# One-hot matrices stored by the attention stage and loaded by the geometric stage, with their scaling on ScalarE

## The chip, the cores and the metric

The kernel runs on one NeuronCore of a Trainium2 chip. The metric is the device time of one execution in microseconds (us), the median of three runs. TensorE (PE) multiplies matrices, VectorE (DVE) and ScalarE (ACT) work elementwise, GpSimd (POOL) issues the gathers, SyncE (SP) issues plain DMAs. Each engine works through its own instructions in order and meets the others at semaphores. PEld in the profile is the weight load of TensorE.

## The reference, cut to what matters

A graph of 3125 nodes and 50000 edges, sorted by destination, goes through two message-passing layers with a feed-forward layer behind each. Both layers sum messages over the edges of each destination node:

```
# layer 0: attention
w   = softmax of scores over the edges of one dst
agg = segment_sum(w * V[src], dst)
# layer 1: geometric
h0, h1 = tensor product of lin(x[src]) with the edge's unit vector
sc   = leaky_relu(h0) @ lsc / 8
act  = softmax(concat([sc, zeros(192)]))        # 64 real logits and 192 zeros
msgs = act * concat([o0, o1])                   # 256 columns for each edge
agg  = segment_sum(msgs, dst)
x    = x + agg
```

## The kernel before, in words

Sorted edges lie in tiles of EP = 128; the edges of one tile all go to one tile of P = 125 nodes. A step takes U = 4 edge tiles, and there are STEPS = 104 steps. A stage sums an edge tile into its node tile by one product on PE: the messages (128 edges x 256 columns) are multiplied by a one-hot matrix (128 edges x 125 nodes) that has a one where the edge's destination is that node. DVE then adds the product to `agg` in SBUF.

`build_attention` is the first of the two stages. Its DVE makes the one-hot matrices of a step with one instruction over 128 x 500 elements (`one_hot`, L1236) into one of two buffers. This happens LAG steps behind the step whose scores it computes. SP loads one 256 KB row block for each step, R = 3 blocks ahead, each after the DVE instruction that frees its buffer (`make`, L1209).

`build_geometric` is the second. For step s, in the order of each engine:

- POOL issues four indirect gathers, 256 KB each, into one of R = 4 buffers `g_rows` (L1418). Before the gathers of step s it waits for `s_xm` of step s - 4.
- DVE, step s: `largest` and `negate` (L1536, L1540) on the logits of s; `projected` for step s + 2 (L1525), which waits for the gathers of s + 2; an addition of step s - 1's product (L1546); `lead` for s + 2 (L1531); an addition; `vec` (L1571), which waits for ACT's exponentials; the sum `rz` (L1577); an addition; `vec` again (L1582); the reciprocal of `rz` (L1585); an addition; `t1` (L1588); the four one-hot matrices of s with the factor `rz` in them (L1593); `msg` columns 0 to 63 (L1596).
- ACT, step s: `turned` for s + 1 (L1429); `exps` for s (L1439, L1441, L1444); `relu` for s + 1 (L1433); `scaled` for s (L1453), which waits for `vec` and ends with `s_xm`.
- PE, iteration s: transposes for s + 1 (L1472); first half of the product of s - 1 (L1500), which waits for `s_msg` and `s_xm` of s - 1; `hidden` for s + 1 (L1477); second half (L1500); `out` for s + 1 (L1486, L1490), on which `largest` of s + 1 waits.

SP has nothing to do in the geometric stage before the change.

Of the kernel before, what the change touches and what calls it, by code (L numbers as in the profile page):

```python
# [25 lines left out]
P = 125  # L26
# [968 lines left out]
def build_attention(nc, m, room):  # L995
# [4 lines left out]
    with ExitStack() as ctx:  # L1000
# [6 lines left out]
        def part(n):  # L1007
# [44 lines left out]
        s_ch = sem("a_ch")  # L1052
        s_w = sem("a_w")
        s_fac = sem("a_fac")
        block = ctx.enter_context(nc.Block())
        LINKS, CHAIN = 5, 18
        (XS, FWD, BWD, ENDS, FIRST, REACH, BACK, LEFT, RIGHT, MINE, DROP, OVER, DIAG, CC, FWD_L, BWD_R, TOP, LESS
         ) = range(1, CHAIN + 1)

# [26 lines left out]

        @block.sync
        def _(sp):
            for s in range(STEPS):
                if s >= R:  # L1090
                    sp.wait_ge(s_ht, s - R + 1)
                sp.dma_start(rowb[s % R][:, :], m.rows_d[s:s + 1, :].to_broadcast([128, 2 * W])
                             ).then_inc(s_row[s % R], 16)

        @block.scalar
        def _(act):
# [107 lines left out]
        def _(dve):  # L1204
# [28 lines left out]
            def one_hot(s):  # L1233
                if s >= 2:
                    dve.wait_ge(s_mm, U * (s - 1))
                dve.tensor_tensor(hot[s % 2][:, :, :], m.iota[:, None, 0:P].to_broadcast([EP, U, P]),  # L1236
                                  m.rec[:, s * U:s * U + U, R_LO:R_LO + 1].to_broadcast([EP, U, P]), ALU.is_equal
                                  ).then_inc(s_hot, 1)
# [121 lines left out]
def build_geometric(nc, m):  # L1360

    MW = D
    R = 4
    AHEAD = 2
    with ExitStack() as ctx:  # L1365
        sem = Sems(nc, ctx)

# [8 lines left out]
        ex = [sb(f"g_ex{b}", [EP, U, 64]) for b in range(2)]  # L1376
        z = [sb(f"g_z{b}", [EP, U]) for b in range(2)]
        en = [sb(f"g_en{b}", [EP, U]) for b in range(2)]
        rz = sb("g_rz", [EP, U])
        t1 = sb("g_t1", [EP, U, 64])  # L1380
        vec = [sb(f"g_vec{b}", [EP, U, 192]) for b in range(2)]
        hot = [sb(f"g_hot{b}", [EP, U, P]) for b in range(2)]
        msg = [sb(f"g_msg{b}", [EP, U, MW]) for b in range(2)]
        xr = sb("g_xr", [EP, U, 64, 3])
        ps_t = ctx.enter_context(nc.psum_tensor("g_pst", [128, U, EP], F32))
# [2 lines left out]
        ps_a = [ctx.enter_context(nc.psum_tensor(f"g_psa{k}", [P, 2, MW], F32)) for k in range(2)]  # L1388
        s_x = [sem(f"g_x_{r}") for r in range(R)]
        s_go = sem("g_go")  # L1390
        s_xr = sem("g_xr")
        s_y = sem("g_y")
        s_tr = sem("g_tr")
# [18 lines left out]
        def _(pool):  # L1412
# [9 lines left out]
            for s in range(STEPS):  # L1422
                gather(s, s % R)

        @block.scalar
        def _(act):
            def turned(s, b):
                act.wait_ge(s_tr, s + 1)
                act.activation(ut[b][:, :, :], ps_t[:, :, :], ACT.Copy).then_inc(s_ut, 1)  # L1429

            def relu(s, b):
                act.wait_ge(s_h, s + 1)
                act.activation(lk[b][:, :, :], ps_h[:, :, :], ACT.Relu).then_inc(s_lk, 1)  # L1433

            def exps(s, b):
                act.wait_ge(s_nm, s + 1)
                if s >= 2:
                    act.wait_ge(s_msg, s - 1)
                act.activation(en[b][:, :], nm[b][:, :], ACT.Exp)  # L1439
                for u in range(U):  # L1440
                    act.activation(ex[b][:, u, :], ps_o[b][:, u, 128:192], ACT.Exp, bias=nm[b][:, u:u + 1],  # L1441
                                   accum_out=z[b][:, u:u + 1])
                for u in range(U):
                    last = act.activation(t1[:, u, :], rows[s % R][:, u, 512:576], ACT.Copy,  # L1444
                                          scale=m.unit2[:, s * U + u:s * U + u + 1])
                last.then_inc(s_ex, 1)

            def scaled(s, b):
                act.wait_ge(s_vec, s + 1)
                if s >= 2:  # L1450
                    act.wait_ge(s_prod, 2 * s - 2)
                for u in range(U):
                    last = act.activation(msg[b][:, u, 64:256], vec[b][:, u, :], ACT.Copy, scale=en[b][:, u:u + 1])  # L1453
                last.then_inc(s_xm, 1)

            turned(0, 0)
            relu(0, 0)
            for s in range(STEPS):
                b = s % 2
                if s + 1 < STEPS:  # L1460
                    turned(s + 1, 1 - b)
                exps(s, b)
                if s + 1 < STEPS:
                    relu(s + 1, 1 - b)
                scaled(s, b)

        @block.tensor
        def _(pe):
            def turn(s, r):
                pe.wait_ge(s_y, s + 1)  # L1470
                for u in range(U):
                    last = pe.transpose(ps_t[:, u, :], rows[r][:, u, 0:128], m.ident[:, :])  # L1472
                last.then_inc(s_tr, 1)

            def hidden(s, b):
                pe.wait_ge(s_ut, s + 1)
                pe.matmul(ps_h.rearrange("p u e -> p (u e)"), m.w_h[:, :],  # L1477
                          ut[b].rearrange("p u e -> p (u e)"), start=True, stop=True).then_inc(s_h, 1)

            def out(s, b):  # L1480
                pe.wait_ge(s_ut, s + 1)
                if s >= 2:
                    pe.wait_ge(s_t1, s - 1)
                    pe.wait_ge(s_ex, s - 1)
                for u in range(U):
                    pe.matmul(ps_o[b][:, u, 0:192], ut[b][:, u, :], m.w_o[:, :], start=u % 2 == 0, stop=False,  # L1486
                              skip_group_check=True)
                pe.wait_ge(s_lk, s + 1)
                for u in range(U):
                    last = pe.matmul(ps_o[b][:, u, 128:192], lk[b][:, u, :], m.w_s[:, :], start=False, stop=True,  # L1490
                                     skip_group_check=True)
                last.then_inc(s_out, 1)

            def aggregate(s, b, k):
                if k == 0:
                    pe.wait_ge(s_msg, s + 1)
                    pe.wait_ge(s_xm, s + 1)
                pe.wait_ge(s_sum, s * U + 2 * k + 2)
                for u in (2 * k, 2 * k + 1):
                    last = pe.matmul(ps_a[k][:, u % 2, :], hot[b][:, u, :], msg[b][:, u, :], start=True, stop=True)  # L1500
                last.then_inc(s_prod, 1)

            turn(0, 0)
            hidden(0, 0)
            out(0, 0)
            for s in range(STEPS + 1):
                b = s % 2
                if s + 1 < STEPS:
                    turn(s + 1, (s + 1) % R)
                if s:  # L1510
                    aggregate(s - 1, 1 - b, 0)
                if s + 1 < STEPS:
                    hidden(s + 1, 1 - b)
                if s:
                    aggregate(s - 1, 1 - b, 1)
                if s + 1 < STEPS:
                    out(s + 1, 1 - b)

        @block.vector
        def _(dve):  # L1520
# [28 lines left out]
            def step(s, r):  # L1549
# [17 lines left out]
                if not last:  # L1567
                    dve.wait_ge(s_ex, s + 1)
                    if s >= 2:
                        dve.wait_ge(s_xm, s - 1)  # L1570
                    dve.tensor_tensor(vec[b].rearrange("p u (c k) -> p u c k", k=3),  # L1571
                                      ps_o[b][:, :, 64:128, None].to_broadcast([EP, U, 64, 3]),
                                      m.unit[:, ds(s * U, U), None, :].to_broadcast([EP, U, 64, 3]), ALU.mult
                                      ).then_inc(s_o01, 1)
                    if s:
                        dve.wait_ge(s_msg, s)
                    dve.scalar_tensor_tensor(rz[:, :], en[b][:, :], 192.0, z[b][:, :], ALU.mult, ALU.add  # L1577
                                             ).then_inc(s_rz, 1)
                add(2)
                if not last:  # L1580
                    dve.wait_ge(s_o01, s + 1)
                    dve.tensor_tensor(vec[b][:, :, :], vec[b][:, :, :], rows[r][:, :, 320:512], ALU.add  # L1582
                                      ).then_inc(s_vec, 1)
                    dve.wait_ge(s_rz, 2 * s + 1)
                    dve.reciprocal(rz[:, :], rz[:, :]).then_inc(s_rz, 1)  # L1585
                add(3)
                if not last:
                    dve.tensor_tensor(t1[:, :, :], t1[:, :, :], ps_o[b][:, :, 0:64], ALU.add).then_inc(s_t1, 1)  # L1588
                    if s >= 2:
                        dve.wait_ge(s_prod, 2 * s - 2)  # L1590
                    dve.wait_ge(s_rz, 2 * s + 2)
                    for u in range(U):
                        dve.tensor_scalar(hot[b][:, u, :], m.iota[:, 0:P], m.rec[:, ds(s * U + u, 1), R_LO],  # L1593
                                          rz[:, u:u + 1], ALU.is_equal, ALU.mult)
                    dve.wait_ge(s_t1, s + 1)
                    dve.tensor_tensor(msg[b][:, :, 0:64], t1[:, :, :], ex[b][:, :, :], ALU.mult).then_inc(s_msg, 1)  # L1596

# [1157 lines left out]
def build(nc, a, out):  # L2755

    m = Memory()
    with ExitStack() as top:
# [10 lines left out]
        m.kv_d = dram("kv_d", [N, 2 * D])  # L2769
        m.n_d = dram("n_d", [N, D])  # L2770
        m.rows_d = dram("rows_d", [STEPS, 2 * U * EP], BF16)
        m.h_d = dram("h_d", [N, D + 256])
        m.h2_d = dram("h2_d", [N, D])
        m.list_d = dram("list_d", [ETX * EP, 3])
# [111 lines left out]
```

## Time and profile before

| | us |
|---|---|
| median of three runs | 3396.8 (3395.88 to 3397.6) |
| profiled execution, its own time | 3404.09 |
| its span in the trace | 3402.4 |
| attention stage, first to last L1209 | 698.9 to 1337.8 |
| geometric stage, first to last L1536 | 1945.86 to 2731.21 |

The profiled execution is 7.3 us above the median, and 1.7 us of its time lie outside the span. In a list of instructions by time, the first column is the start, the second the duration; several equal instructions in a row are merged, and then the duration reaches from the first one's start to the last one's end. Square brackets give how long the engine had been idle and what released it; gaps under about 0.15 us have no bracket. In the slices of the page each digit is a fortieth of the span (85 us).

### The profile page before, as it was taken

The page shows a single profiled execution, that of the slowest core. Times are in us where ns is not written, and L with a number is a line of the kernel's source. Part 1 is how long each engine was busy: PE and PEld are TensorE (multiplying, and loading weights), DVE is VectorE, ACT ScalarE, POOL GpSimd, SP SyncE. Part 2 cuts the span into 40 slices and gives each one's busy share as a digit, 9 for nine tenths or more (in the row PEclk, how much of TensorE's full clock was granted, in tenths as well). Part 3 has the DMA queues.
Part 4 walks back from the last instruction along what each step waited for, and adds up shares of the span by engine and source line. Part 5 has one row for each costly group of instructions (what it writes and reads, how often), then busy time and mean ns, then how long its engine had stood idle before and what let it go on. Part 6 is the DMA issues. An engine that isn't in the chain of part 4 may idle for free. (4 is left out here: it accounts for less than half of the span.)

```text
span 3402.4 us, 46710 instructions
## 1 busy us (share of the span) xinstructions
PE 2523.4 (74%) x13323; PEld 1876.0 (55%) x13323; DVE 2327.2 (68%) x5588; ACT 1251.8 (37%) x4625; POOL 1438.7 (42%) x1404
## 2 busy tenths in 40 slices
PE   6666666257777777342993488888888869999997
PEld 3545545134545544132773355555555558889997
DVE  8766666289999999347773299999999962022221
ACT  1000000016666666401220166666666632233332
POOL 0677777266656554000000155545555403434432
PEclk9956666568988889775996699999999969999999
DMA  4343333767666666411000445444544452222223
GB/s 110 79 113 88 88 88 93 46 223 218 206 201 205 204 201 157 91 30 27 1 1 4 125 140 143 134 141 137 142 138 138 129 155 87 64 53 38 36 38 65
DMA packets 263912, 371.97 MB, mean 109 GB/s; under 512 B 115207, under 2 KB 176533, under 8 KB 263346
## 3 DMA queue, kind: packets, MB, share of 16 engines
q0 software_dynamic: 91456, 234.61, 26.1%
q1 hardware_dynamic: 139950, 129.91, 14.2%
q10 hardware_dynamic: 32260, 4.51, 1.3%
q8 instruction: 114, 1.87, 0.2%
q14 instruction: 132, 1.08, 0.1%
HBM read 334.75 MB, written 37.20 MB: 109 GB/s over the span
## 5 line engine op out<-in xcount | busy, mean ns | idle before, releaser
L1418 POOL DMA_INDIRECT g_rows<-h_d,src x416 | 403.3, 969 | 969.7 <-SPq L1365 588.0
L1082 POOL DMA_INDIRECT a_strip<-kv_d,src x416 | 404.6, 972 | 305.7 <-DVE x L1218 131.8
L332 POOL DMA_INDIRECT rec_d<-o_rec_in,o_place x392 | 399.9, 1020 | 219.8 <-issue 113.0
L1106 ACT ACTIVATE x<-a_strip,x 128x64 f32<-128x64 f32 x1664 | 408.4, 334 | 138.3 <-PE a_psv L1151 138.2
L1151 PE MATMUL a_psv<-x 128*125 128x260 f32 x832 | 290.4, 454 | 125.2 <-DVE agg L1248 115.0
L1500 PE MATMUL g_psa<-g_msg,g_hot 128*125 128x256 f32 x832 | 253.1, 430 | 123.6 <-DVE g_msg L1596 123.6
L1500 PEld LDWEIGHTS g_psa<-g_msg,g_hot 128*125 128x125 f32 x832 | 148.8, 199 | 262.0 <-DVE g_msg L1596 148.5
L1151 PEld LDWEIGHTS a_psv<-x 128*125 128x125 f32 x832 | 143.9, 206 | 205.5 <-DVE agg L1248 176.0
L416 PE MATMUL o_ps_base<-o_run,o_lo_hot_t 125*128 125x26 f32 x782 | 162.8, 360 | 120.7 <-DVE o_run L546 120.7
L1453 ACT ACTIVATE g_msg<-g_vec,g_en 128x192 f32<-128x192 f32 x416 | 155.1, 443 | 210.0 <-DVE g_vec L1582 210.0
L2369 DVE TENSOR_TENSOR e_w1s<-e_psy,e_room 128x256 f32<-128x256 f32 x56 | 23.8, 425 | 291.3 <-PE e_psy L2572 291.3
L416 PEld LDWEIGHTS o_ps_base<-o_run,o_lo_hot_t 125*128 125x128 f32 x782 | 151.0, 288 | 130.4 <-DVE o_run L546 130.4
L1131 PE MATMUL a_psq<-q,a_ht 125*128 x1248 | 203.5, 317 | 21.5 <-DVE a_ht L1209 15.6
L2560 PE MATMUL e_psh<-e_w1s,e_h_t 128*128 128x128 f32 x1792 | 209.3, 275 | 0.0
L2572 PE MATMUL e_psy<-e_w,e_w2s 128*128 x896 | 204.3, 382 | 4.8 <-DMA e_w<-in_L_ffn_W2p 4.8
L2463 POOL DMA_INDIRECT x_d<-e_w1s,e_listed x56 | 110.1, 1965 | 226.0 <-DVE e_w1s L2371 213.9
L2560 PEld LDWEIGHTS e_psh<-e_w1s,e_h_t 128*128 128x128 f32 x1792 | 204.6, 192 | 0.2
L1248 DVE TENSOR_TENSOR agg<-agg,a_psv 125x260 f32 x416 | 172.8, 415 | 24.5 <-PE a_psv L1151 20.7
L1546 DVE TENSOR_TENSOR agg<-agg,g_psa 125x256 f32 x416 | 170.0, 409 | 28.3 <-PE g_psa L1500 27.2
L1131 PEld LDWEIGHTS a_psq<-q,a_ht 125*128 125x128 bf16 x1248 | 134.8, 109 | 85.2 <-issue 39.8
L2572 PEld LDWEIGHTS e_psy<-e_w,e_w2s 128*128 128x128 f32 x896 | 167.2, 192 | 25.7 <-issue 5.0
L2642 ACT ACTIVATE e_w2s<-e_psh,e_b 128x128 f32<-128x128 f32 x448 | 127.7, 368 | 122.4 <-PE e_psh L2560 122.4
(423 smaller groups left out, 5347.2 us busy)
## 6 DMA issues: line engine op xcount, KB each, us to landing
a_row<-rows_d SPq DMA_DIRECT2D x104, 256.0 KB
o_row<-dst_rows_d SPq DMA_DIRECT2D x98, 256.0 KB, 4.3
o_row_lo<-lo_rows_d SPq DMA_DIRECT2D x98, 128.0 KB, 4.6
e_w<-in_L_ffn_W1p SPq DMA_DIRECT2D x8, 1024.0 KB
e_w<-in_L_ffn_W2p SPq DMA_DIRECT2D x8, 1024.0 KB
a_strip<-kv_d,src POOLq DMA_INDIRECT x416
g_rows<-h_d,src POOLq DMA_INDIRECT x416
rec_d<-o_rec_in,o_place POOLq DMA_INDIRECT x392
```

The lines of the kernel that those rows point to most:

```text
L332: pool.indirect_dma_start(out=m.rec_d[:, :], out_offset=bass.IndirectOffsetOnAxis(ap=place[s % RP][:, u:u + 1], axis=0), in_=rec_in[:, U * ...
L416: last = pe.matmul(ps_base[b][:, u * NH:(u + 1) * NH], lo_hot_t[b][0:P, u, :], table, start=True, stop=True)
L1082: pool.indirect_dma_start(out=strip[:, lane.start + u, place:place + 2, :].rearrange("p a d -> p (a d)"), out_offset=None, in_=m.kv_d[:, : ...
L1106: act.activation(msg[b][:, u, h, 0:HD], strip[:, lane.start + u, place, h * HD:(h + 1) * HD], ACT.Copy, scale=w[:, k * U + u, h:h + 1])
L1131: last = pe.matmul(ps_q[b][:, u, :], ht[b][0:P, u * EP:(u + 1) * EP], m.q[:, j, k, :], start=k == 0, stop=k == 2)
L1151: pe.matmul(ps_v[u % 2][:, 0:H * HW], hot[b][:, u, :], msg[b][:, u, :, :].rearrange("p h d -> p (h d)"), start=True, stop=True).then_inc(s ...
L1248: dve.tensor_tensor(agg, agg, ps_v[u % 2][:, 0:H * HW], ALU.add).then_inc(s_add, 1)
L1418: pool.indirect_dma_start(out=rows[r][:, u, 64:576], out_offset=None, in_=m.h_d[:, :], in_offset=bass.IndirectOffsetOnAxis(ap=m.src[:, s * ...
L1500: last = pe.matmul(ps_a[k][:, u % 2, :], hot[b][:, u, :], msg[b][:, u, :], start=True, stop=True)
L1546: dve.tensor_tensor(m.agg[:, j, :], m.agg[:, j, :], ps_a[u // 2][:, u % 2, :], ALU.add).then_inc(s_sum, 1)
L2560: last = pe.matmul(ps_h[b][:, c * EP:(c + 1) * EP], own[b][:, k, c * 128:(c + 1) * 128], xt[b][:, k, :], start=k == 0, stop=k == 1)
L2572: last = pe.matmul(ps_y[b][:, 0:D], ht[b][:, c, :], w2[:, e, c, :], start=c == 0, stop=c == NF - 1)
```

## The change

The attention stage stores each step's one-hot matrices (unscaled, 256 KB of f32) to a new DRAM tensor `hot_d`, issued by SP. The geometric stage no longer makes them: SP loads them into a ring of four buffers, and ACT multiplies each by `rz` behind the scaling of `msg`, ahead of `s_xm`. `rz` gets a second buffer.

```diff
 # build_attention
+        s_kept = [sem(f"a_kept{b}") for b in range(2)]
+        KEEP = LAG + R
         @block.sync
-            for s in range(STEPS):
-                if s >= R:
-                    sp.wait_ge(s_ht, s - R + 1)
-                sp.dma_start(rowb[s % R][:, :], m.rows_d[s:s + 1, :].to_broadcast([128, 2 * W])
-                             ).then_inc(s_row[s % R], 16)
+            for s in range(STEPS + KEEP):
+                if s < STEPS:
+                    if s >= R:
+                        sp.wait_ge(s_ht, s - R + 1)
+                    sp.dma_start(rowb[s % R][:, :], m.rows_d[s:s + 1, :].to_broadcast([128, 2 * W])
+                                 ).then_inc(s_row[s % R], 16)
+                v = s - KEEP
+                if v >= 0:
+                    sp.wait_ge(s_hot, v + 1)
+                    sp.dma_start(m.hot_d[v], hot[v % 2]).then_inc(s_kept[v % 2], 16)
+            for b in range(2):
+                sp.wait_ge(s_kept[b], 16 * len(range(b, STEPS, 2)))
             def one_hot(s):
                 if s >= 2:
                     dve.wait_ge(s_mm, U * (s - 1))
+                    dve.wait_ge(s_kept[s % 2], 16 * (s // 2))
 # build_geometric
+    RH = 4
-        rz = sb("g_rz", [EP, U])
+        rz = [sb(f"g_rz{b}", [EP, U]) for b in range(2)]
-        hot = [sb(f"g_hot{b}", [EP, U, P]) for b in range(2)]
+        hot = [sb(f"g_hot{r}", [EP, U, P]) for r in range(RH)]
+        s_hot = [sem(f"g_hot_{r}") for r in range(RH)]
+        @block.sync
+        def _(sp):
+            for s in range(STEPS):
+                if s >= RH:
+                    sp.wait_ge(s_prod, 2 * (s - RH) + 2)
+                sp.dma_start(hot[s % RH][:, :, :], m.hot_d[s]).then_inc(s_hot[s % RH], 16)
         # ACT, scaled(s, b)
                 for u in range(U):
-                    last = act.activation(msg[b][:, u, 64:256], vec[b][:, u, :], ACT.Copy, scale=en[b][:, u:u + 1])
+                    act.activation(msg[b][:, u, 64:256], vec[b][:, u, :], ACT.Copy, scale=en[b][:, u:u + 1])
+                h = hot[s % RH]
+                act.wait_ge(s_hot[s % RH], 16 * (s // RH) + 16)
+                act.wait_ge(s_rz, 2 * s + 2)
+                for u in range(U):
+                    last = act.activation(h[:, u, :], h[:, u, :], ACT.Copy, scale=rz[b][:, u:u + 1])
                 last.then_inc(s_xm, 1)
         # PE, aggregate(s, b, k)
-                    last = pe.matmul(ps_a[k][:, u % 2, :], hot[b][:, u, :], msg[b][:, u, :], start=True, stop=True)
+                    last = pe.matmul(ps_a[k][:, u % 2, :], hot[s % RH][:, u, :], msg[b][:, u, :], start=True, stop=True)
         # DVE, step(s, r)
-                    if s:
-                        dve.wait_ge(s_msg, s)
-                    dve.scalar_tensor_tensor(rz[:, :], en[b][:, :], 192.0, z[b][:, :], ALU.mult, ALU.add
+                    dve.scalar_tensor_tensor(rz[b][:, :], en[b][:, :], 192.0, z[b][:, :], ALU.mult, ALU.add
                                              ).then_inc(s_rz, 1)
...
-                    dve.wait_ge(s_rz, 2 * s + 2)
-                    for u in range(U):
-                        dve.tensor_scalar(hot[b][:, u, :], m.iota[:, 0:P], m.rec[:, ds(s * U + u, 1), R_LO],
-                                          rz[:, u:u + 1], ALU.is_equal, ALU.mult)
 # build
+        m.hot_d = dram("hot_d", [STEPS, EP, U, P])
```

## Rows read from the trace of the kernel before

**Rows 1.** The page, busy tenths of VectorE in forty slices.
```profile
DVE  8766666289999999347773299999999962022221
```

**Rows 2.** Busy time by stretch: attention, geometric stage, then its first step and three later ones.
```profile
1200.00:1300.00 100.00, 76.72 (x513) 49.29 (x513) 98.37 (x179) 63.18 (x267) 61.02 (x63) 0.91 0.69 206
2400.00:2500.00 100.00, 85.56 (x411) 58.72 (x409) 96.78 (x243) 64.25 (x252) 50.00 (x53) 0.97 0.51 142
...
1945.86:1954.79 8.93, 7.41 (x26) 4.69 (x26) 6.03 (x14) 6.32 (x21) 1.90 (x2) 0.65 0.36 107
2395.11:2403.47 8.36, 7.71 (x30) 4.68 (x30) 7.29 (x19) 4.89 (x20) 3.80 (x4) 0.80 0.46 128
2403.47:2410.71 7.24, 6.11 (x30) 4.27 (x30) 7.21 (x19) 4.89 (x20) 3.81 (x4) 1.00 0.52 145
```

**Rows 3.** The instructions on `g_mx`, one a step: durations, first and last start.
```profile
L1536 DVE TENSOR_REDUCE g_mx<-g_pso x104: 411/418/424, 1945.9 to 2731.2; 128x4 f32<-128x256 f32 x104
```

**Rows 4.** Groups of instructions, 2000 to 2700 us: busy, mean ns, idle before.
```profile
L1593 DVE TENSOR_SCALAR g_hot<-iota,rec,g_rz 128x125 f32<-128x125 f32 x370 | 102.1, 340 | 0.0
L1444 ACT ACTIVATE g_t<-g_rows,unit 128x64 f32<-128x64 f32 x368 | 97.7, 350 | 0.0
L1453 ACT ACTIVATE g_msg<-g_vec,g_en 128x192 f32<-128x192 f32 x369 | 137.7, 443 | 185.1 <-DVE g_vec L1582 185.1
```

**Rows 5.** One step and a half by time, 2403.4 to 2419 us.
```profile
2403.61 1.13 PE L1500 MATMUL g_psa<-g_msg,g_hot 128*125 128x256 f32 x4 [0.65 <-DVE g_msg L1596]
...
2404.00 0.96 DVE L1525 TENSOR_TENSOR g_xr<-g_rows,unit 128x768 f32<-128x768 f32 x1
2404.13 0.20 ACT L1439 ACTIVATE g_en<-g_nm 128x4 f32<-128x4 f32 x1 [0.54 <-DVE g_nm L1540]
2405.39 1.06 ACT L1444 ACTIVATE g_t<-g_rows,unit 128x64 f32<-128x64 f32 x4
2406.49 0.96 DVE L1571 TENSOR_TENSOR g_vec<-g_pso,unit 128x768 f32<-128x768 f32 x1
2408.03 1.10 PE L1490 MATMUL g_pso<-w_s,g_lk 64*128 64x64 f32 x8
2408.75 1.50 ACT L1453 ACTIVATE g_msg<-g_vec,g_en 128x192 f32<-128x192 f32 x4 [1.82 <-DVE g_vec L1582]
2409.36 1.11 DVE L1593 TENSOR_SCALAR g_hot<-iota,rec,g_rz 128x125 f32<-128x125 f32 x4
2410.15 0.58 ACT L1429 ACTIVATE g_ut<-g_pst 128x512 f32<-128x512 f32 x1
2410.38 0.42 DVE L1596 TENSOR_TENSOR g_msg<-g_t,g_ex 128x256 f32<-128x256 f32 x1
2410.71 0.42 DVE L1536 TENSOR_REDUCE g_mx<-g_pso 128x4 f32<-128x256 f32 x1
2411.03 0.95 POOL L1418 DMA_INDIRECT g_rows<-h_d,src  x1 [2.52 <-ACT g_msg L1453]
2411.36 0.96 DVE L1525 TENSOR_TENSOR g_xr<-g_rows,unit 128x768 f32<-128x768 f32 x1
2414.79 0.95 POOL L1418 DMA_INDIRECT g_rows<-h_d,src  x1 [0.31 <-issue]
2416.01 1.49 ACT L1453 ACTIVATE g_msg<-g_vec,g_en 128x192 f32<-128x192 f32 x4 [1.83 <-DVE g_vec L1582]
```

**Rows 6.** The last gather of a step, and the DVE instruction that waited for it.
```profile
2536.87 0.95 POOL L1418 DMA_INDIRECT g_rows<-h_d,src  x1 [0.31 <-issue]
...
2540.56 0.96 DVE L1525 TENSOR_TENSOR g_xr<-g_rows,unit 128x768 f32<-128x768 f32 x1 [2.20 <-DMA g_rows<-h_d,src]
```

**Rows 7.** Attention, 700 to 1300 us, the group on which gathers are waited for.
```profile
L1218 DVE TENSOR_TENSOR x<-a_strip,a_psr 128x1024 f32<-128x1024 f32 x96 | 116.3, 1212 | 3.3 <-DMA a_strip<-kv_d,src 3.2
```

**Rows 8.** The page, DMA issues: a 256 KB load and its time to landing.
```profile
o_row<-dst_rows_d SPq DMA_DIRECT2D x98, 256.0 KB, 4.3
```

More of the change, by code:

```diff
@@ L1584, in step @@
                     dve.wait_ge(s_rz, 2 * s + 1)
-                    dve.reciprocal(rz[:, :], rz[:, :]).then_inc(s_rz, 1)
+                    dve.reciprocal(rz[b][:, :], rz[b][:, :]).then_inc(s_rz, 1)
                 add(3)
```

## The prediction

> **What bounds the kernel now.** I read the page's slices first: DVE stands at 9 in two stretches, which are the attention and the geometric stage [rows 1]. Busy time by stretch gives these their numbers: 98.4% and 96.8% for DVE, with ACT at 63% and 64% [rows 2]. That invites the reading "DVE is full, ACT has room, so move work from one to the other". Two things have to be checked before it holds: how far DVE can shrink before something else sets the step, and where in ACT's order the work lands.
>
> The geometric stage runs from 1945.9 to 2731.2 us, 785.35 us for 103 steps, 7.62 us each [rows 3]. A plain step takes 7.24 us at a granted clock of 1.00; 70 of the 103 lie below 7.4. In 18 steps the clock granted to PE falls for a part of the step (0.80 in one shown) and the step takes about 8.36, so 1.12 more, 20 us in all [rows 2]. Of the 39.6 us above 103 x 7.24 the remaining 19 are late gathers (one is shown in [rows 6], with DVE idle for 2.20 us) and the slow start.
>
> In the plain step the list by time shows DVE without gaps, but for one: at 2411.36 L1525 starts 0.65 us after L1536 at 2410.71, though the two small instructions ahead of it took 0.53 in the step before (2403.47 to 2404.00). I read the 0.12 as gathers that had only just landed [rows 2, 5]. So a second loop is nearly as long as DVE's own work. It goes: ACT ends `scaled` of s (`s_xm`), POOL gathers s + 4, L1525 in step s + 2 takes it, DVE goes on to L1582, ACT scales s + 2. In numbers, all [rows 5] unless said:
> - L1525 to the start of `scaled` of its step, DVE in order: 2411.36 to 2416.01, 4.65.
> - `scaled`: 1.49.
> - its end to POOL's first gather: 2408.75 + 1.50 = 2410.25 to 2411.03, 0.78.
> - first to last gather: 2411.03 to 2414.79, 3.76.
> - last gather's start to L1525 where this had waited: 2536.87 to 2540.56, 3.69 [rows 6].
>
> Sum 14.37 for two steps, 7.19 a step, against 7.24 of DVE. Both bind at once.
>
> **The change part by part.**
> *Taken from DVE.* Four instructions with mean 340 ns [rows 4], but overlapped: L1593 to the next instruction is 2409.36 to 2410.38, 1.02 us a step [rows 5]. DVE alone would come to 6.22. The wait on `s_msg` that goes and the two `rz` buffers cost nothing; the order of DVE met it anyway.
>
> *Added to ACT.* Four ACTIVATEs of 128x125 with a scale from memory; before has none of this size with this form. The nearest rows are 128x64 and 128x192, also with such a scale. Four of 64 columns take 1.06 from first start to last end with a mean of 0.350, so (1.06 - 0.35)/3 = 0.237 from start to start; four of 192 take 1.49 with 0.443, so 0.349 [rows 4, 5]. By columns, 125 lie at 0.237 + 61/128 x 0.112 = 0.290, four 1.16. Bounds: 4 x 0.237 = 0.95 and 4 x 0.349 = 1.40. I take 1.16, between two near rows. ACT has the time (its idle before L1453 is 1.8 us a step, 185.1 in all [rows 4, 5]), but that idle lies ahead of `scaled`, and the new work stands behind it.
>
> *Where this goes.* `s_xm` comes 1.16 later, and three things hang on it.
> 1. The gather loop: 14.37 + 1.16 = 15.53 for two steps, **7.77** a step (7.67 and 7.89 by the bounds).
> 2. A loop of one step through ACT's order, which had slack before. `scaled` of s to `turned` 1.40 (2408.75 to 2410.15); new scalings 1.16; `turned` 0.58, less about 0.10 of overlap, 0.48; `exps` of s + 1, 2404.13 to 2405.39 + 1.06, 2.32; to L1571 0.04; L1571 to `scaled` 2.26. Sum **7.66** [rows 5]; without the scalings 6.50, under 7.24, which is why nobody sees it before.
> 3. PE: products of s start 1.16 later. First product to the end of `out` is 2403.61 to 2409.13, 5.5 us, after `s_xm` of that step; DVE's L1536 needs it about 7.7 us after. It is two microseconds early, so no bound; these two microseconds also soften the clock's dips.
>
> So a plain step goes from 7.24 to about 7.8: the freed 1.02 us of DVE become a wait for `g_rows` ahead of L1525 or for `exps` ahead of L1571. I take 7.80, a little over the longer loop, since gathers land unevenly and either loop may be the late one in a given step. 103 x 0.56 = 57.7 us.
>
> *The loads of `hot_d`.* 256 KB a step on top of 1 MB of gathers. SP waits for the product of s - 4, four steps ahead, while a load of this size lands in 4.3 us [rows 8]; never late. But it shares the DMA engines with the gathers, whose landing is now on the path. They are 52% busy in 7.24 us with 1 MB, so 256 KB are at most 0.94 us; wholly ahead of the last gather that is 0.47 a step, at least 0. I take 0: they are half idle, and the load's four steps of notice let it fall anywhere.
> The Trainium skill (DMA: Bandwidth & Descriptors, "Anatomy of one DMA") gives a gather of this size 2.0 us plus bytes over 436 GB/s, an estimate of 2.6 from issue to landing. [rows 6] show 3.69, and the trace decides; with 2.6 the gather loop would be 7.22, the loop through ACT, 7.66, would set the step, and the time would be 3433, still inside the range below.
>
> *Attention.* Each step adds a 256 KB store. DVE's new wait is for a store issued two steps earlier, over 11 us before, against 4.3 for a transfer of such size [rows 8]. SP is now held at `s_hot`, so the next row load goes out later, but still over a step and a half (about 8 us) ahead of its use. The gathers there are issued three steps ahead; DVE waited 3.2 us for them in 600 [rows 7], at a DMA share of 0.69 that rises by about 0.15 [rows 2]. Cost 0; if row loads were late by 0.5 us a step, 52 us. Behind the last store nothing waits that is not longer than it.
>
> *Dips and stalls.* The late gathers stay (they now find no slack), 19 us as before. The dips cost 20 us before; PE's two microseconds hide some, but the first product feeds an addition that DVE needs directly, so I give back 7 of the 20, between 0 and 20.
>
> Sum: +57.7 - 7 = **+51 us**. On the profiled execution, 3404 to 3455; on the median of 3396.8, **3448**.
>
> **The rivals.**
> - *Transfers crowd.* Gathers land up to 0.94 later, the loop is 8.24: 103 x 0.44 more than 7.80, 45, so 3493. For it: both now start from the same PE and ACT events. Against it: half-idle DMA engines. Chance 0.12.
> - *The clock.* With longer pauses PE may be granted less. Attention has 0.91 at 77% busy PE, the geometric stage 0.97 at 86%; at 0.65 a step took 8.93 [rows 2]. Half the steps like that would add 51 x 1.1 = 56, giving 3504. After the change PE is about 79% busy, like attention, which argues against it. Chance 0.06. The Trainium skill (TensorE: Matmul & The Clock Gate, "What's actually happening") has activity release the throttle; the first step's 0.65 agrees.
> - *Attention pays*: 3500, as above. Chance 0.05.
> - *Faster, other side.* ACT's scalings cost little beyond DVE's gain: if the gather loop is not on the path (`s_xm` late is hidden) and ACT takes the scalings in the 1.8 us in which it idles, the step falls to what DVE and PE need, 6.22. 103 x 1.02 = 105 less: 3292. It decides where gather loop and ACT loop are both under 7.24, that is where the added time is under 0.10 resp. 0.74 us; the instruction order speaks against it. Chance 0.06.
> - *Nothing moves*: the 0.56 and dips all returned or gathers returning sooner once fewer DVE instructions run. Within 0.2% (7 us, about what a measurement of this kernel can tell). 3397. Chance 0.04.
>
> **The numbers.** The forecast has 0.67. Its own range: low, both bounds for ACT low (7.67), all dips hidden: 103 x 0.43 - 20 = +24, 3421; high, 7.89 plus half the crowding, 0.24: +91, 3488. With a little of the neighbours outside, the range is 3415 to 3488. Slower 0.90 (forecast and three rivals), same 0.04, faster 0.06.
>
> **What would show it.** In the profile after: L1536 to L1536 about 7.8 in plain steps; DVE busy near 80% in the geometric stage, idle ahead of L1525 `<-DMA g_rows` or L1571 `<-ACT g_t` at some 1.5 us a step; ACT near 79%, its gap ahead of L1453 nearly as before; four 128x125 ACTIVATEs in about 1.2 us; POOL's first gather 0.8 after the last of them; attention's ends unchanged within 5 us. A step under 7.24 makes the loops wrong; gathers landing over 4.2 us after the last issue make it the crowding.

## The result, and the profile after

The changed kernel takes 3486.7 us (median of four) against 3396.3: ratio 1.0272, 95% interval 1.0250 to 1.0293, slower. The forecast was slower by 51 us, 3448, with a range of 3415 to 3488. The way was right, the size was not: 90 us, at the range's upper edge.

The view of one instruction per step, of the changed kernel (durations, then first and last start), and of the DVE instruction that reads SP's row loads in attention:

```profile
L1560 DVE TENSOR_REDUCE g_mx<-g_pso x104: 424/425/426, 1936.8 to 2806.4; 128x4 f32<-128x256 f32 x104
```
```profile
L1218 DVE TENSOR_SCALAR a_ht<-a_row,part x104: 465/479/702, 690.4 to 1328.8; 128x1024 bf16<-128x1024 bf16 x104
```

Attention takes 638.4 us from first to last, as before (638.9). The geometric stage takes 869.6 against 785.35 [rows 3]: +84.2 us. The spans of the two profiled executions differ by only 75.6 (3478.0 against 3402.4); in the changed one attention starts 8.5 us earlier, at 690.4, behind work that the change does not touch. Busy groups of the changed kernel, 2000 to 2700 us (busy and mean ns; idle before and releaser):

```profile
L1549 DVE TENSOR_TENSOR g_xr<-g_rows,unit 128x768 f32<-128x768 f32 x83 | 80.1, 965 | 95.2 <-DMA g_rows<-h_d,src 95.2
L1570 DVE TENSOR_TENSOR agg<-agg,g_psa 125x256 f32 x332 | 135.7, 409 | 50.5 <-PE g_psa L1524 49.7
L1472 ACT ACTIVATE g_msg<-g_vec,g_en 128x192 f32<-128x192 f32 x332 | 123.9, 443 | 176.9 <-DVE g_vec L1604 176.9
L1477 ACT ACTIVATE g_hot<-g_hot,g_rz 128x125 f32<-128x125 f32 x332 | 103.9, 384 | 0.0
```

ACT's idle ahead of `msg` is still there (176.9 us in 83 steps, 2.1 each; 185.1 in 92, 2.0 each, before [rows 4]): the new scalings did not go into it. DVE idles instead of working, 95 us for gathers (`g_rows`) and 50 for products (`g_psa`). It almost never waits for ACT's exponentials: 2.8 us, twice, in the whole stage.

Four stretches of the changed kernel; those from 2401.03 on are one step each. Columns: length, busy time of PE, PEld, DVE, ACT and POOL, granted PE clock, DMA share, GB/s.

```profile
2401.03:2409.18 8.15, 6.08 (x30) 4.27 (x30) 6.36 (x14) 5.84 (x24) 4.58 (x4) 1.00 0.57 174
2409.18:2418.12 8.94, 7.47 (x30) 4.86 (x30) 6.59 (x14) 5.93 (x24) 3.81 (x4) 0.81 0.56 170
2418.12:2425.90 7.78, 6.25 (x32) 4.26 (x30) 6.46 (x15) 5.83 (x24) 4.22 (x4) 1.00 0.43 121
```

The plain step is 7.78, where 7.77 was worked out and 7.80 taken. But it is not the usual one: of 103 steps 35 take 7.7 to 7.9 us and 46 take over 8.8, mostly 8.98, often every second one. In them the clock falls for a part of the step, as in the 18 steps of 8.36 before [rows 2]. A third kind, like the first row, has a full clock and yet 0.4 more. By time, the same stretch of the changed kernel:

```profile
2401.16 1.25 ACT L1477 ACTIVATE g_hot<-g_hot,g_rz 128x125 f32<-128x125 f32 x4
2403.25 0.96 DVE L1549 TENSOR_TENSOR g_xr<-g_rows,unit 128x768 f32<-128x768 f32 x1 [1.58 <-DMA g_rows<-h_d,src]
2405.64 0.95 DVE L1595 TENSOR_TENSOR g_vec<-g_pso,unit 128x768 f32<-128x768 f32 x1
2405.71 0.95 POOL L1430 DMA_INDIRECT g_rows<-h_d,src  x1 [0.30 <-issue]
2406.91 0.95 DVE L1604 TENSOR_TENSOR g_vec<-g_vec,g_rows 128x768 f32<-128x768 f32 x1
2406.97 1.72 POOL L1430 DMA_INDIRECT g_rows<-h_d,src  x1 [0.30 <-issue]
2410.65 2.04 PE L1524 MATMUL g_psa<-g_msg,g_hot 128*125 128x256 f32 x4 [2.06 <-issue]
2412.84 0.42 DVE L1570 TENSOR_TENSOR agg<-agg,g_psa 125x256 f32 x1 [0.52 <-PE g_psa L1524]
```

Two things to see. PE pauses for 2.06 us ahead of its first product (0.65 before [rows 5]), and that product then takes 2.04 instead of 1.13, so the addition that DVE needs comes late. (The median of this pause over all steps is 1.70 us, and 1.30 in the plain ones; before it was 1.13.) And POOL's fourth gather takes 1.72 us to issue instead of 0.95: it starts 0.06 us after L1604. The gather that starts just as close behind L1595 takes 0.95. Such issues of over 1.1 us number 60 in the stage, 12 before.

### The profile page after: what moved, and what is told of

It is laid out like the page before. It is cut to its first block and busy times, and to the rows that moved or that the text cites. A ratio compares the mean times of both kernels' runs of the same rounds, so it can differ in the third digit from the quotient of the medians.

```text
span 3478.0 us, 47126 instructions
## 1 busy us (share of the span) xinstructions
PE 2549.9 (73%) x13323; PEld 1881.4 (54%) x13323; DVE 2248.0 (65%) x5172; ACT 1361.4 (39%) x5041; POOL 1462.6 (42%) x1404
## 3 DMA queue, kind: packets, MB, share of 16 engines
q1 hardware_dynamic: 169902, 183.17, 19.4%
## 5 line engine op out<-in xcount | busy, mean ns | idle before, releaser
L1430 POOL DMA_INDIRECT g_rows<-h_d,src x416 | 428.3, 1030 | 1028.0 <-POOLq L74 587.6
L1524 PE MATMUL g_psa<-g_msg,g_hot 128*125 128x256 f32 x832 | 272.1, 457 | 172.1 <-issue 166.9
L1524 PEld LDWEIGHTS g_psa<-g_msg,g_hot 128*125 128x125 f32 x832 | 160.3, 214 | 327.3 <-issue 211.3
L1549 DVE TENSOR_TENSOR g_xr<-g_rows,unit 128x768 f32<-128x768 f32 x104 | 100.2, 964 | 121.3 <-DMA g_rows<-h_d,src 121.3
```

Source lines behind the costliest of these rows:

```text
L1430: pool.indirect_dma_start(out=rows[r][:, u, 64:576], out_offset=None, in_=m.h_d[:, :], in_offset=bass.IndirectOffsetOnAxis(ap=m.src[:, s * ...
L1524: last = pe.matmul(ps_a[k][:, u % 2, :], hot[s % RH][:, u, :], msg[b][:, u, :], start=True, stop=True)
```

## The experiments

Two theories for the 33 us of the stage that the forecast of 51 lacked: the **clock** (PE's longer pause lets it fall), or **transfers** (loads of `hot_d` and slow gathers). The geometric stages of the main runs stand in one table at the end of this section, each from one profiled execution. The runs from fill3 to gap_vec stood beside a kernel before of about 3400 us; the last four beside one of about 3580. There attention and the sort were longer in all kernels, the plain geometric step was again 7.24 and 7.8, so for these the ratio and the stage are compared, not the median.

### fill3: the pause filled

```diff
-                for u in range(U):
-                    last = pe.transpose(ps_t[:, u, :], rows[r][:, u, 0:128], m.ident[:, :])
+                for u in range(U * 3):
+                    last = pe.transpose(ps_t[:, u % U, :], rows[r][:, u % U, 0:128], m.ident[:, :])
```

> The changed kernel, with each step's four transposes issued three times instead of once (same result, same place). That is 8 x 0.137 = 1.1 us of TensorE work in the pause of about 2 us that it now makes ahead of each first product. Clock theory (plain steps are 7.8 as forecast, and the rest of the loss is that the longer pause lowers the granted clock in about every second step, which then takes 8.98): the clock of the geometric stage rises from 0.90 to 0.95 or more and the time falls by 25 to 55 us against the changed kernel. Transfer theory (the loads of hot_d and GpSimd's longer issues make the long steps): nothing changes, or it is up to 5 us slower.

Measured: 3458.2 us, ratio 1.0183 (1.0157 to 1.0210), 28 us less than the changed kernel, by doing 832 needless transposes. (Twelve transposes take 1.53 us where four take 0.66, so they fill 0.87 us of a step and not the 1.1 of the expectation.) The whole stage, fill3, then the changed kernel:

```profile
1938.00:2780.80 842.80, 719.05 (x3906) 529.82 (x3905) 656.22 (x1436) 600.79 (x2366) 423.89 (x403) 0.99 0.53 157
```
```profile
1936.80:2806.40 869.60, 701.91 (x3082) 463.61 (x3082) 663.22 (x1437) 605.48 (x2366) 413.92 (x402) 0.90 0.50 152
```

The clock rises from 0.90 to 0.99 and 27 us go; steps over 8.8 fall from 46 to 9, and steps with a clock under 0.95 from 47 to 3. The clock theory holds for this part. But the mean step is 8.18, not 7.8: about 40 us over plain steps remain at a full clock, and DVE waits 140 us for gathers. Something else is there.

### no_loads: without the loads of hot_d

```diff
-            for s in range(STEPS):
-                if s >= RH:
-                    sp.wait_ge(s_prod, 2 * (s - RH) + 2)
+            for s in range(RH):
                 sp.dma_start(hot[s % RH][:, :, :], m.hot_d[s]).then_inc(s_hot[s % RH], 16)
...
-                    last = act.activation(h[:, u, :], h[:, u, :], ACT.Copy, scale=rz[b][:, u:u + 1])
+                    last = act.activation(hot_s[b][:, u, :], h[:, u, :], ACT.Copy, scale=rz[b][:, u:u + 1])
```

> The changed kernel without the step-by-step loads of hot_d in the geometric stage: four blocks are loaded once, and ScalarE scales them into two buffers of their own, so that the sums are over wrong one-hot matrices while all engine work stays. Transfer theory: the long steps go and the time falls by 25 to 40 us. Clock theory: long steps stay, within 8 us of the changed kernel (a little may come from GpSimd's issues, 60 of which took over 1.1 us against 12 before, 25 us in sum, most of it off the path).

The lines left out give the products the new buffers. The sums are over wrong one-hot matrices, with all engine work kept.

Measured: 3486.1 us, ratio 1.0265, the changed kernel's time; the stage 869.5 at a clock of 0.90, while the DMA share falls from 0.50 to 0.44. The loads cost nothing, and the long gather issues (75) are not theirs. The transfer theory in this form falls.

### free_early: only the gather loop shortened

```diff
-                    act.activation(msg[b][:, u, 64:256], vec[b][:, u, :], ACT.Copy, scale=en[b][:, u:u + 1])
+                    last = act.activation(msg[b][:, u, 64:256], vec[b][:, u, :], ACT.Copy, scale=en[b][:, u:u + 1])
+                last.then_inc(s_free, 1)      # and the gathers wait for s_free
```

> The changed kernel, but GpSimd's gathers wait for a semaphore of their own that ScalarE raises behind the scaling of msg and ahead of the one-hot scalings. The gather loop goes from 7.77 to 7.19 and the loop through ScalarE's order (7.66 forecast, about 7.75 with scalings of 1.25 us) sets the step. By that sum: plain steps 7.7, a few us to 10 us faster than the changed kernel, waits of L1549 on gathers gone, waits of the vec instruction on ScalarE in their place. If the gather loop alone were the cause, the time would return to the kernel before or better, about 85 us less.

Measured: 3474.4 us, ratio 1.0229, 12 us less. The most frequent step is again 7.7 to 7.9 (53 steps), and 41 still take 8.8 to 9.1. So the gather loop is not the only one of its length, and alone it gives back little. In its plain steps DVE hardly waits for gathers any more (0.04 us in the median, 0.48 in the changed kernel) but for the first product (1.09 us), and the step stays 7.78. With the gather loop at 7.19 and ACT's order at 7.66 by the prediction's own sum, that is a third loop; the last experiment shows it.

### store_only: attention alone

Its edit is the attention part of the change, with `build_geometric` as before.

> The kernel before with the attention stage of the changed kernel (the stores of hot_d, read by nobody). Both theories: within 5 us of before. If attention pays for row loads that come later, up to 50 us slower; then the stage from first to last L1218 is longer than 638 us.

Measured: 3399.2 us, ratio 1.0008 (0.9991 to 1.0024). The stores are free here, though the DMA share of attention (700 to 1300 us) rises from 0.71 to 0.82; the stage takes 638.6 us, as before.

### before_fill2 and before_vec: the same two losses in the kernel before

```diff
-                for u in range(U):                       # before_fill2: each transpose twice
+                for u in range(U * 2):
```
```diff
-                    pool.wait_ge(s_xm, s - R + 1)        # before_vec: gathers released by DVE's L1582
+                    pool.wait_ge(s_vec, s - R + 1)
```

> The kernel before with its four transposes issued twice (0.55 us more TensorE work in the pause of 0.65 to 1.4 us ahead of the first product). Clock theory: the 21 dips of the geometric stage go and the time falls by up to 20 us, 10 to 20. If the dips are not set by TensorE's pauses: unchanged, or slower by up to 10 us.

> The kernel before, but the gathers of step s wait for the last reader of their buffer on VectorE (s_vec of s - 4) instead of ScalarE's end of scaled. Gather loop 14.37 - 1.5 = 12.9 for two steps, 6.4 a step. If the gathers share the bound with VectorE, as the prediction says: waits on gathers (12 us in the stage) go, plain steps come to VectorE's own 7.15 to 7.24, 10 to 25 us faster. If gathers never bound: no change.

Measured: 3383.2 us, ratio 0.9957 (0.9942 to 0.9973), and 3382.8, 0.9954 (0.9937 to 0.9971): 15 us each, and 19.1 and 16.9 in the stage. Both losses were there before the change, about as the prediction had them (20 us and 19). before_vec removes all 6 steps over 8.8 us but leaves the plain step at 7.24: there the gather loop bound only where gathers were late, and DVE's own work set the plain step.

### gap and gap_vec: the scalings moved into ScalarE's idle time

```diff
 # DVE: rz and its reciprocal ahead of the first vec instruction
+                    dve.scalar_tensor_tensor(rz[b][:, :], en[b][:, :], 192.0, z[b][:, :], ALU.mult, ALU.add
+                                             ).then_inc(s_rz, 1)
+                    dve.wait_ge(s_rz, 2 * s + 1)
+                    dve.reciprocal(rz[b][:, :], rz[b][:, :]).then_inc(s_rz, 1)
 # ACT, scaled(s, b): the four one-hot scalings first, then
+                act.wait_ge(s_vec, s + 1)
+                for u in range(U):
+                    last = act.activation(msg[b][:, u, 64:256], vec[b][:, u, :], ACT.Copy, scale=en[b][:, u:u + 1])
                 last.then_inc(s_xm, 1)
 # left out: the same lines at their old places, which go
 # gap_vec alone: gathers released by s_vec
```

> The changed kernel with rz and its reciprocal made ahead of vec on VectorE, and ScalarE's one-hot scalings moved ahead of the scaling of msg, into the 1.8 us in which it waits for vec. Loop through ScalarE's order: back to about 6.5, s_xm no longer 1.16 later. Gather loop 7.19 plus stalls sets the step: 7.2 to 7.5 on plain steps, 3380 to 3420, near the kernel before. If the added ScalarE work as such is the cost, wherever it stands: no better than the changed kernel.

> The same as gap, and the gathers released by s_vec as in before_vec. Gather loop about 6.4, VectorE's work 6.2, ScalarE's and TensorE's about 6.3: steps of 6.4 to 6.9, 75 to 110 us faster than the kernel before. If something else holds the step (pauses that lower the clock, gather issues held up by VectorE), 7.0 to 7.4 and 20 to 50 us faster.

Measured: gap 3408.2 us, ratio 1.0034 (1.0018 to 1.0051); gap_vec 3359.4, ratio 0.9892 (0.9865 to 0.9919), faster than both kernels. The same work of ACT costs 78 us less at the other place (82 in the stage). By time, gap_vec:

```profile
2400.98 1.27 ACT L1474 ACTIVATE g_hot<-g_hot,g_rz 128x125 f32<-128x125 f32 x4 [0.16 <-PE g_psa L1524]
2401.95 0.95 DVE L1606 TENSOR_TENSOR g_vec<-g_vec,g_rows 128x768 f32<-128x768 f32 x1
2402.94 1.49 ACT L1477 ACTIVATE g_msg<-g_vec,g_en 128x192 f32<-128x192 f32 x4 [0.69 <-DVE g_vec L1606]
```

The scalings run while DVE makes `vec`, and 0.69 us of idle is left. gap_vec did not reach the 75 to 110 us of the expectation but its second range, 20 to 50: 41 steps take 6.6 to 7.0, but the mean is 7.22. Part of the miss is DVE's work, busy 668.5 us in 103 steps, 6.49 each and not 6.2. What fills the rest was not taken apart; its gather issues over 1.1 us number 72.

### fill3_psum: the long gather issues

```diff
-                    dve.tensor_tensor(vec[b][:, :, :], vec[b][:, :, :], rows[r][:, :, 320:512], ALU.add
+                    dve.tensor_tensor(vec[b][:, :, :], vec[b][:, :, :], ps_o[b][:, :, 0:192], ALU.add
```

> fill3, but the second addition to vec (L1604) takes its second operand from PSUM (ps_o, same shape and size) instead of SBUF (rows), so it adds wrong numbers. Port theory (a gather's issue that starts while VectorE runs an instruction with two SBUF inputs is held until that instruction ends): the issues that start inside L1604 take 0.95 us as all others (in fill3 41 of 46 took more, 1.45 in the mean), those inside L1549 still take 1.4; the time falls by 5 to 20 us against fill3. If the long issues come from anything else (DMA queues, full rings): as many as in fill3, same time.

Measured: 3641.2 us beside 3577.1, ratio 1.0170 (1.0145 to 1.0195). By time, fill3_psum:

```profile
2311.46 0.95 DVE L1604 TENSOR_TENSOR g_vec<-g_vec,g_pso 128x768 f32<-128x768 f32 x1
2311.91 0.95 POOL L1430 DMA_INDIRECT g_rows<-h_d,src  x1 [0.30 <-issue]
```

The gather starts inside L1604 and is issued in 0.95 us. Counted over the whole traces: of the issues that start inside L1604, 42 of 65 took over 1.1 us in fill3 and 0 of 65 here; of those inside L1549, which still has both inputs in SBUF, 31 of 63 and 39 of 67. (The others start in the last third of the instruction, or within 0.04 us of its start.) L1595, of the same size but with one input in PSUM, holds none of 71 in fill3. The operand makes the long issue. In time: the stage is 832.5 us against 842.8, 10 less, in one execution of each; the ratios, 1.0170 and 1.0183, do not tell the two apart, so the price of the long issues is not shown. The Trainium skill (SBUF — State Buffer, "SBUF: two separate sides") says that a VectorE instruction with two SBUF inputs and a GpSimd one that reads SBUF exclude each other: whichever starts first holds the shared ports for its whole instruction. These counts agree.

### The two fixes together: before_vec_fill2, gap_vec_fill2, after_vec_fill3

Their edits are those above, combined; after_vec_fill3 is the changed kernel with `s_vec` and the transposes three times.

> The kernel before with both single edits that made it faster (gathers released by s_vec, transposes issued twice). If the clock's dips and the gathers' lateness are separate losses, the two gains of 15 us add up: 25 to 30 us faster than before, steps of 7.24 nearly throughout (104 x 7.24 = 753 us for the stage against 785). If they are the same loss: 15 to 18.

> gap_vec with the transposes issued twice. Its trace still has 12 dips of the clock: 5 to 10 us faster than gap_vec by the clock theory. If TensorE is by now near the bound (its work is about 6.1 of 6.8 us in the short steps, and 0.55 is added), slower by 5 to 20 us.

> The changed kernel with gathers released by s_vec and the transposes issued three times, so that neither the gathers nor the clock should set the step; ScalarE's one-hot scalings stay where the change put them. What is left is the loop through ScalarE's order, forecast as 7.66 and 7.75 with the measured 1.25 us of scalings: a stage of 103 x 7.75 = 798 us with most steps within 0.1 of each other, 45 to 50 us longer than the kernel before with the same two edits (749). If ScalarE's order is not a loop of its own: steps of 7.2 to 7.4 and a stage of 750 to 765.

Measured: ratios 0.9916 (0.9893 to 0.9939), 0.9897 (0.9874 to 0.9920) and 1.0062 (1.0043 to 1.0081). The two gains add up in before_vec_fill2: 749 us, 97 of 103 steps at 7.2 to 7.3. In gap_vec_fill2 the clock is at 0.99 but the stage only 3 us shorter than gap_vec's, so its dips cost less than expected. Stages of before_vec_fill2 and after_vec_fill3:

```profile
2122.10:2871.10 749.00, 673.71 (x3494) 483.65 (x3494) 739.38 (x1848) 500.35 (x1958) 391.06 (x402) 1.00 0.51 142
```
```profile
2124.60:2929.40 804.80, 717.18 (x3894) 530.05 (x3894) 657.75 (x1436) 604.29 (x2366) 419.45 (x400) 0.99 0.58 163
```

In after_vec_fill3 neither the clock nor the gathers set the step, and 92 of 103 steps take 7.7 to 7.9. One of them, by time, from one first product to the next:

```profile
2493.52 1.10 PE L1524 MATMUL g_psa<-g_msg,g_hot 128*125 128x256 f32 x4 [0.84 <-issue]
2494.76 0.42 DVE L1570 TENSOR_TENSOR agg<-agg,g_psa 125x256 f32 x1 [1.19 <-PE g_psa L1524]
2498.55 1.50 ACT L1472 ACTIVATE g_msg<-g_vec,g_en 128x192 f32<-128x192 f32 x4 [1.93 <-DVE g_vec L1604]
2499.95 1.26 ACT L1477 ACTIVATE g_hot<-g_hot,g_rz 128x125 f32<-128x125 f32 x4
2501.31 1.10 PE L1524 MATMUL g_psa<-g_msg,g_hot 128*125 128x256 f32 x4 [0.84 <-issue]
```

This is a loop of one step that closes: first product to its addition 1.24, DVE in order to the scaling of `msg` 3.79, `msg` to the one-hot scalings 1.40, these to the next first product 1.36, together 7.79. DVE idles ahead of that addition, 1.18 us in the median, and nowhere from there to L1604, in 88 of 90 plain steps. The expectation had the loop through ACT's order instead, at 7.75. It has slack: ACT's last exponential instruction (L1463) ends 0.16 us ahead of L1595, against 0.03 in the kernel before, so this loop is about 7.66. In the changed kernel too DVE waits for the first product in 28 of 34 plain steps, so the loop through the product sets these as well.

| geometric stage, us | as it is | transposes repeated | gathers released early | both |
|---|---|---|---|---|
| one-hots on DVE | 785.3 | 766.2 | 768.4 | 749.0 |
| one-hots on ACT behind `msg` | 869.6 | 842.8 | 857.2 (free_early, behind `msg`) | 804.8 |
| one-hots on ACT ahead of `msg` | 787.6 | not run | 743.6 | 740.2 |

## Why the prediction was wrong in size

The table splits the 84.2 us in two. Down its last column, the plain steps: 804.8 - 749.0 = **+56**. The rest is what clock dips and late gathers cost together: 869.6 - 804.8 = 64.8 where they cost 785.3 - 749.0 = 36.3, **+28.5**. The last column ran beside the slower kernel before.

How the 28.5 divides is not shown, because the order of the edits decides it. Transposes first: the clock 26.8 where it was 19.1, +7.7, then the gathers 38.0 where they were 17.2, +20.8. Gathers first: 12.4 where they were 16.9, -4.5, then the clock 52.4 where it was 19.4, +33.0. (free_early releases a little later than `s_vec`, so this order is not quite the same edit.) The two losses overlap: with gathers released early, the 46 steps with a clock under 0.95 still take 8.97 us in the mean, and the others 7.80.

- *The reading of before*: right in the main. Plain steps were DVE's own; the gather loop, a little under it, bound only where gathers were late (before_vec: 15 us, plain step unchanged).
- *DVE gives 1.02 a step*: too much, though worth nothing where the scalings stand behind `msg`. DVE is busy 78.3 us less in the stage (741.5 to 663.2), 0.76 a step, in part because the instructions around the gap overlap less: L1614 starts 0.51 us behind L1610 (2408.18 to 2408.69), which it reads, where L1593 had started 0.34 behind L1588. DVE alone would be about 6.5, not 6.22.
- *The scalings, 1.16 us*: right. Four take 1.25 from first start to last end, but the first starts 0.10 before `msg` ends and the next instruction of ACT starts 1.15 to 1.16 behind the first (2401.16 to 2402.31 in the changed kernel), so they delay `s_xm` and ACT's order by 1.16.
- *The plain step, 7.80, +57.7*: right in size, 7.78 and +56, and right that the place behind `msg` is the reason: ahead of it the same work costs 78 us less. But the loop that sets the step was not in the sum, so the size is part luck. The prediction had 7.77 for gathers and 7.66 for ACT's order; the loop through the first product and its addition is 7.79.
- *Loads and stores at 0*: right, by no_loads and store_only.
- ***Dips and stalls*, the step that failed.** It said that the late gathers stay at 19 us and that 7 of the dips' 20 come back, 32 together. They cost 64.8 together where they had cost 36.3: instead of -7 it was +28.5. The reason stands in item 3 of *Where this goes*: PE is "two microseconds early, so no bound; these two microseconds also soften the clock's dips". That was reckoned to L1536, which needs `out`. DVE needs the first product's addition much sooner, and with `s_xm` 1.16 later this path has no slack at all. So PE spends its spare time waiting ahead of the product (2.06 us in the step shown), the clock falls in 47 steps instead of 25, and what a dip adds to the product is on the path: in the step at 2409.18 the addition comes 2.19 us behind the product's start (2410.65 to 2412.84), 0.94 more than in plain steps, and the step is 1.16 longer than the plain one. This is the clock rival's mechanism, beside the forecast and not instead of it, at 8 to 33 us by the two orders where the rival had 56. The profile had a hint: attention, with PE busy 77%, had 0.91 [rows 2], and the prediction took the likeness as an argument against.
- *"The late gathers stay at 19"* belongs to the same term. In fill3, at a full clock, late gathers cost 38.0 and DVE waits 140 us for them: a gather loop of 7.77 has no slack beside 7.79, and the shifted phase put POOL's issues inside L1549 and L1604 so that 60 were long instead of 12. The sum had no term for the phase. fill3_psum shows what makes an issue long; what the long ones cost it does not show.

Sum: the plain steps +56 for 57.7, the dips and late gathers +28.5 for -7, so 84 for 51.

## What to carry to other kernels

Work moved to an idle engine is only free if it stands where that engine idles: look at which side of its wait the new instructions land, and what is released by the semaphore behind them. Before costing an offload, sum every loop that passes through the receiving instruction, with buffers' release and gather latency in it; here three loops, 7.66, 7.77 and 7.79, lay within 0.13 us of each other, and the longest was the one not summed: judge an engine's slack at the first of its results that somebody needs, not at its last. And a loss that is hidden by slack (a clock dip, a held issue) has to be priced again when the change takes the slack away.

## What the runs showed of the hardware

- Needless TensorE work made both kernels faster: 832 transposes more, 28 us less (clock 0.90 to 0.99); in the kernel before 416 more, 15 us less (0.94 to 0.99). They shorten the pause ahead of the first product from 1.70 to 1.16 us in the median, and from 1.13 to 0.69.
- An indirect gather's issue takes 0.95 us on POOL. If it starts inside a VectorE instruction with two SBUF inputs (more than 0.04 us and less than about 0.7 behind its start), it ends 0.83 us after that instruction does: 1.72 for one that starts 0.06 behind it (2406.97 against 2406.91). With the second input in PSUM, 0.95. An issue that is already under way when such an instruction starts takes 0.95 too.
